# Value products of two key tiles in a row, with sixteen buffers for exponentials, in the attention stages with small heads

## The reference, cut to what matters

```python
scores = jnp.einsum('bhqd,bhkd->bhqk', q, k) * scale      # + mask, or slopes and causal
attn   = jax.nn.softmax(scores, axis=-1)
out    = jnp.einsum('bhqk,bhkd->bhqd', attn, v)
```

## The kernel before, in words

| stage | keys | key tiles `nkt` | small | score banks for the maxima `A_BANKS` |
|---|---|---|---|---|
| pyr_coarse | 512 in blocks of 256, 128, 128 | 4 | yes | 3 |
| pyr_core | 512 | 4 | yes | 3 |
| l1x_core | 1024 | 8 | yes | 3 |
| l2a_core | 512 | 4 | yes | 3 |
| la_core | 1536 | 12 | no | 3 |
| l3a_core | 512, causal | 4 | yes | 3 |
| l3x_core | 1024, masked | 8 | yes | 2 |

## Time and profile before

### The profile page before, as it was taken

The page is one execution under the profiler, slowest core; times in us unless marked ns, Lnnn a source line. Parts: engine busy times, 40 slices in busy tenths (PEclk is TensorE's granted clock), DMA queues, the critical chain, the costliest instruction groups (busy, mean ns, idle before and its releaser), DMA issues. The chain is left out here.

```text
span 5453.5 us, 72915 instructions
## 1 busy us (share of the span) xinstructions
PE 4470.3 (82%) x20471; PEld 2052.5 (38%) x20471; DVE 3008.7 (55%) x6900; ACT 2794.5 (51%) x5841; POOL 1691.7 (31%) x1362
## 2 busy tenths in 40 slices
PE   8779663847799956794898899999998869669986
PEld 5322553745322255323343233333334544312223
DVE  4567564036488522677653555555552247558875
ACT  3447221322366722472444477777774226339993
POOL 2112141121201111121442477777775111300001
PEclk9679876978799977896999899999999889769998
DMA  8544102520823254542545544444430055644421
GB/s 301 137 106 111 54 2 63 189 79 1 283 52 95 56 202 157 175 111 85 184 175 195 128 105 100 102 103 109 109 91 18 34 161 129 206 132 108 109 62 37
DMA packets 534966, 634.87 MB, mean 116 GB/s; under 512 B 84644, under 2 KB 441748, under 8 KB 522180
## 3 DMA queue, kind: packets, MB, share of 16 engines
q1 hardware_dynamic: 527168, 595.62, 38.7%
q0 software_dynamic: 6384, 32.61, 1.9%
q10 hardware_dynamic: 1068, 2.66, 0.2%
HBM read 399.52 MB, written 217.45 MB: 113 GB/s over the span
## 5 line engine op out<-in xcount | busy, mean ns | idle before, releaser
L828 POOL TENSOR_TENSOR la_core_weight_sums<-la_core_weight_sums,la_core_weights 128x1024 f32<-128x1024 f32 x320 | 752.3, 2351 | 140.2 <-ACT la_core_weights L693 132.6
L734 DVE TENSOR_REDUCE la_core_part_max<-ps 128x1 f32<-128x512 f32 x768 | 518.9, 681 | 499.6 <-PE ps L560 499.0
L630 PE MATMUL ps<-la_core_q,la_core_k 128*128 128x512 bf16 x2304 | 624.5, 382 | 13.5 <-ACT ps L676 10.3
L693 ACT ACTIVATE la_core_weights<-ps 128x512 f32<-128x512 f32 x768 | 455.5, 593 | 293.3 <-PE ps L630 293.3
L218 POOL TENSOR_TENSOR proj_parts<-proj_rest,proj_parts 128x512 bf16<-128x512 f32 x240 | 303.8, 1273 | 663.5 <-ACT proj_parts L169 663.0
L676 ACT ACTIVATE ps<-la_core_tops 128x512 f32<-128x512 f32 x768 | 460.3, 599 | 57.9 <-DMA la_core_tops<-la_core_max_rows 57.9
L593 PE MATMUL ps<-la_core_weights,la_core_v 128*64 128x512 f32 x1536 | 414.0, 617 | 0.0
L630 PEld LDWEIGHTS ps<-la_core_q,la_core_k 128*128 128x128 bf16 x2304 | 195.0, 98 | 485.1 <-ACT ps L676 302.5
L734 DVE TENSOR_REDUCE l1x_core_part_max<-ps 128x1 f32<-128x512 f32 x512 | 316.7, 681 | 83.7 <-PE ps L558 77.1
L206 DVE CAST proj_parts<-proj_full 128x512 bf16<-128x512 f32 x240 | 168.0, 700 | 313.8 <-ACT proj_full L181 158.2
L730 DVE CUSTOM_DVE_ANT_0 l3x_core_unused<-ps,l3x_core_mask_q 128x512 f32<-128x512 f32 x512 | 330.6, 686 | 7.4 <-DVE l3x_core_row_max L738 4.9
(11 more groups left out here) (460 smaller groups left out, 8487.2 us busy)
## 6 DMA issues: line engine op xcount, KB each, us to landing
la_core_k<-latent_k_parts SPq DMA_DIRECT2D x128, 384.0 KB
latent_k_parts<-proj_parts SPq DMA_DIRECT2D x96, 384.0 KB, 2.6
cf_w<-in_L1f_w SPq DMA_DIRECT2D x32, 1024.0 KB, 6.9
values<-proj_value SPq DMA_DIRECT2D x112, 256.0 KB, 3.1
latent_values<-proj_value SPq DMA_DIRECT2D x96, 256.0 KB, 3.0
la_core_q<-latent_q_parts SPq DMA_DIRECT2D x192, 128.0 KB
la_core_v<-latent_values SPq DMA_DIRECT2D x32, 768.0 KB, 5.5
k_parts<-proj_parts SPq DMA_DIRECT2D x56, 384.0 KB, 2.6
```

The lines of the kernel that those rows point to most:

```text
L630: mm = nc.tensor.matmul(out, k_stack[r][:, kp, j, ks], q_stack[r][:, p, j, qs], start=False, stop=False, skip_group_check=True)
L693: nc.scalar.activation(weights[:, (g * NS + s) % WEIGHTS, qs], k.ps[:, B0 + (g * NS + s) % B_BANKS, qs], ACT.Exp, scale=scale).then_inc(ex ...
L734: nc.vector.reduce_max(out, scores, AX).then_inc(a_taken, 1)
L828: nc.gpsimd.tensor_tensor(total, total, own, ALU.add).then_inc(added, 1)
```

## The change

In the stages with small heads the value products of two key tiles are issued one behind the other: behind the key tiles 2, 4, 6 of a group stand those of tiles 0 and 1, 2 and 3, 4 and 5, and behind the first key tile of the next group those of its last two tiles. `weights` has 16 buffers there in place of 8, 16 KB more in each partition. `copy_sums` stands behind the second key tile's exponentials in place of the first's. `out_rows` of the pyramid is allocated after pyr_core, and its transfer (256 KB read as a broadcast) moves from the projection before pyr_coarse to SyncE's part of the first level merge, which now waits for it. la_core is as it was.

```diff
-    WEIGHTS = 8
+    WEIGHTS = 16 if small else 8
+    together = 2 if small else 1
     ahead_tiles = WEIGHTS // heads
...
-                    if i:
-                        weigh(b, g, i - 1)
-                    elif exists(*later(b, g, -1)):
-                        weigh(*later(b, g, -1), nkt - 1)
+                    if i and i % together == 0:
+                        for tile in range(i - together, i):
+                            weigh(b, g, tile)
+                    elif i == 0 and exists(*later(b, g, -1)):
+                        for tile in range(nkt - together, nkt):
+                            weigh(*later(b, g, -1), tile)
                     if i == 0 and exists(*later(b, g, 1)):
                         turn(*later(b, g, 1))
...
-            weigh(B - 1, groups - 1, nkt - 1)
+            for tile in range(nkt - together, nkt):
+                weigh(B - 1, groups - 1, tile)
...
-                    if s == heads - 1 and exists(*later(b, g, -1)):
+                    if s == together * heads - 1 and exists(*later(b, g, -1)):
                         copy_sums(*later(b, g, -1))
...
-def merge_levels_stage(k, lvl, att, up, out_w, up_w, out_b, up_b, up_next, value_bias):
+def merge_levels_stage(k, lvl, att, up, out_w, up_w, out_b, up_b, up_next, value_bias, loads=()):
...
         def _(sync):
             k.clear_last_set(sync)
+            for tile, source in loads:
+                sync.dma_start(tile, source).then_inc(loaded, 16)
+            if loads:
+                sync.wait_ge(loaded, 16 * len(loads))
...
-        prefetch += [(out_rows[:], inp["L0_out_b0_up_b0"].partition_broadcast(P)), (out_b[:], inp["L0_out_b"]), (up_b[:], inp["L0_up_b"]),
-                     (vbias[:], inp["L0_v_b"])]
+        prefetch += [(out_b[:], inp["L0_out_b"]), (up_b[:], inp["L0_up_b"]), (vbias[:], inp["L0_v_b"])]
...
+        out_rows = sb("rows", [P, 2, C])
...
-                               up_b[:, min(lvl, 2), :], up[i + 1], vbias[:, lvl, :])
+                               up_b[:, min(lvl, 2), :], up[i + 1], vbias[:, lvl, :],
+                               loads=[(out_rows[:], inp["L0_out_b0_up_b0"].partition_broadcast(P))] if i == 0 else ())
```

More of the change, by code:

```diff
@@ L1023, in merge_levels_stage @@
         nc.sbuf_tensor(f"level_bias_{lvl}", [P, CH], F32) as level_bias,
-        k.stage("values_biased", "bias_sum", "ready", "summed", "quartered", "upsampled") as (
-            values_biased, bias_sum, ready, summed, quartered, upsampled),
+        k.stage("values_biased", "bias_sum", "ready", "summed", "quartered", "upsampled", "loaded") as (
+            values_biased, bias_sum, ready, summed, quartered, upsampled, loaded),
         nc.Block(no_gpsimd_drain=True) as block,
@@ L1088, in pyramid_attention @@
         xs = k.xT[:].rearrange("p c (b s) -> p c b s", b=B)
-        out_w, up_w, out_rows = sb("out_w", [P, 4, CH, C]), sb("up_w", [P, 3, CH, C]), sb("rows", [P, 2, C])
+        out_w, up_w = sb("out_w", [P, 4, CH, C]), sb("up_w", [P, 3, CH, C])
         out_b, up_b = sb("out_b", [P, 4, CH]), sb("up_b", [P, 3, CH])
         prefetch = [(out_w[:, lvl], inp["L0_out_w"][lvl]) for lvl in range(4)] + [(up_w[:, lvl], inp["L0_up_w"][lvl]) for lvl in range(3)]
-        prefetch += [(out_rows[:], inp["L0_out_b0_up_b0"].partition_broadcast(P)), (out_b[:], inp["L0_out_b"]), (up_b[:], inp["L0_up_b"]),
-                     (vbias[:], inp["L0_v_b"])]
+        prefetch += [(out_b[:], inp["L0_out_b"]), (up_b[:], inp["L0_up_b"]), (vbias[:], inp["L0_v_b"])]
         with nc.sbuf_tensor("pyr_wqkv", [P, 4, CH, 3 * C], F32) as w, nc.sbuf_tensor("pyr_zeros", [P, H * QUAD], F32) as zeros:
```

## The result

| | before | after |
|---|---|---|
| median | 5449.86 us (5443.2 to 5451.83, 4 runs) | 5605.7 us (5603.56 to 5611.34, 4 runs) |
| profiled execution | 5453.5 us | 5605.8 us |
| ratio | | 1.0289, 95% interval 1.0275 to 1.0304 |

The change makes the kernel 2.9% slower. The forecast was 5561 us with a range of 5500 to 5600: the direction came as forecast, but the time lies 45 us above the forecast and 6 above the range. The next table sets the terms of the forecast's sum against the two traces; a stage is taken here from the start of its first exponential to the start of its last.

A forecast was written before the change was run, and what follows sets the result against it. TensorE's order was taken as the bound, VectorE close behind, ScalarE in l3x. pyr_core 18, l2a 18, l1x 26, l3x 39, pyr_coarse 4 and l3a 6 give 111 us: 5450 + 111 = 5561 us, range 5500 to 5600.

The forecast's parts named there:

- The bound: Six changed stretches: TensorE's order bounds five, with VectorE 87% full close behind in l1x; ScalarE bounds l3x.
- the switches: On TensorE, switching to value products and back costs 0.24 us; the change saves one in two.
- VectorE's banks: In l1x, eight-pair runs wait for VectorE's three banks: 0.49 us lost, 0.24 saved, so +0.25 us a pair.
- the timetable: l1x chunk starts from the first pass S: last chunk 3.78 us, value products 4.09, next run 5.94.
- Rival 1: Faster: TensorE's order is the bound, only switches count; 160 pairs save 38 us, giving 5412 us; chance 0.07.
- The change of group: A group's first chunk loses its value product cover: pyr_core's pair there +0.98 us, group +1.23; l1x group +1.75.
- Rival 3: The group change costs nothing more, its wait overlapping VectorE's idle time: 5520 us; chance 0.15.
- The term of +39 us: l3x: 1.5 us a group for pairs plus 1.1 at the group change, over 15 groups.
- The last groups, left out: Last two of 16 groups, without pass A: 15 groups counted; range allows up to 2 us for each of 12.
- pyr_coarse and l3a: Additional value products lengthen the wait for the maxima's row: +4 us in pyr_coarse, +6 in l3a.
- The rest at nothing: Exponentials' buffers, `copy_sums` and the moved transfer in the first level merge: 0 us, the transfer at most 2.
- l3x's banks: Upper bound in l3x: VectorE's two banks add another 0.25 us a pair, 15 us more.

The follow-up runs named there:

- VectorE relieved: Changed kernel, VectorE reading only half of each score chunk for its maxima in small-head stages: 5499.47 us; the kernel before with the same halving: 5380.33 us.
- The kernel with single edges: Changed kernel with the value products of a group's last two key tiles issued one at a time, pairs only inside a group: 5524.69 us, ratio 1.0127.
- the kernel that has all fillers: Changed kernel plus redundant score products in l3x: six per group change, two before chunks 8, 16, 24, one behind each last-two-groups pass S product: 5567.0 us.
- the six fillers: Six redundant score products before each l3x group's first pass A chunk: 5586.15 us in the changed kernel, 5454.88 us in the kernel before.
- the relaxed kernel: Changed kernel whose first pass A chunks of a group wait only for the maximum that last used their bank: 5575.03 us, ratio 1.0234.

## Why the prediction was right, and where it was wrong

**The bound, the switches, VectorE's banks: right outside l3x.** Two tiles in a pair take 5.96 us in l1x where they took 5.69, forecast 5.94, and the timetable holds chunk by chunk. With VectorE relieved the pair takes 5.45, which is the switch's 0.24 alone. Rival 1 had the price right and the bound wrong.

**The change of group: right.** 12.83 to 12.92 us in pyr_core (12.9 forecast) and 24.9 to 25.0 in l1x (24.95). The kernel with single edges shows that most of it hangs on the lost cover (0.9 of 1.2 us). Rival 3 falls.

**l3x: this is the step that failed.** The term of +39 us measured +81.9, because the sum priced TensorE's products in l3x at full clock and put the clock's part at nothing. The forecast took "0.5 us a pair, 3 x 0.5 = 1.5 a group" and, at the change of group, "removing that cover of 1.00 adds as much, with some 0.1 more". At full clock both came: 7.47 us a pair, and 31.23 to 31.24 us a group where fillers held the clock. What is missing is the price of waits beyond their own length: two waits of 0.9 us a group became eight of 3.7, and the clock fell to 0.88. Set out with the kernel that has all fillers:

| l3x, us | before | after, all fillers | after |
|---|---|---|---|
| first to last transpose (15 groups) | 441.4 | 478.8 | 509.0 |
| last transpose to last exponential | 54.2 | 58.0 | 68.5 |
| stage | 469.0 | 510.2 | 550.9 |
| clock | 0.97 | 0.98 | 0.88 |

(The first transpose comes 26.6 us ahead of the first exponential in each.) The order is worth 510.2 - 469.0 = 41 us, against 39 forecast; the lost clock 550.9 - 510.2 = 41 us, against none. The split has a fringe: the six fillers cost 4.8 us by themselves in the kernel before, and what the fillers cost after counts here as order. Without any filler, the two groups of the relaxed kernel give about the same price a group: 3.2 us between a clock of 1.00 and one of 0.90. Of the clock's 41 us, 30 lie in the groups with a pass A and 10.5 in the last two groups.

Could it have been seen? The wait of 0.99 us in the earlier trace rows and a granted clock that fell three times in l3x, the last time behind waits of 0.5 to 1.1 us, were both in the trace of before. The forecast itself made the wait of 0.99 into 2.1 us (it measured 1.59), added others behind it, and expected TensorE's busy share to fall, and then priced all products of l3x at the duration they had at full clock.

**The last groups, left out: a smaller miss.** "The last two of 16 groups have no pass A; what they cost there [...] I leave out" was meant to be worth up to 2 us for each such group, so 4 a stage. It was 5 in l1x (41.6 from the last transpose to the last exponential in place of 36.6) and 3.8 in l3x at full clock. Pairs cost there too: 5.27 us in l1x where two tiles took 4.92, 7.53 in l3x where they took 7.0.

**pyr_coarse and l3a: a little too high.** In pyr_coarse the waits for the row rose by 1.0 us in all. pyr_coarse's 31.9 us and l3a's 5.2 became:

```profile
PE ps L627 <- DMA pyr_coarse_q<-pyr_coarse_max_parts: 32.9, 15, 4.4
```

```profile
PE ps L627 <- DMA l3a_core_q<-l3a_core_max_parts: 11.5, 11, 2.7
```

In l3a the wait rose by 6.3 us, as forecast, but the stage only by 2.5, and by 1.1 to 5.9 if the other traces with pairs are set against this one before. Something may have been given back beside the wait. The saved switches are a candidate, which the forecast had ruled out as a gain; no run isolates them there.

**The rest at nothing: right**, as far as 0.15% can show. The kernel with buffers and transfer alone is at 0.9994 (0.9985 to 1.0004).

**The sum.** Of the 42.5 us by which the stages exceed the forecast, l3x has 42.9, l1x 4.1 and pyr_core 1.2; l3a, pyr_coarse and l2a take back 5.4. The upper end of the range allowed 15 us more for l3x's banks and 24 for the last groups, but nothing for the clock. That the total missed the range by only 6 us is due to these allowances, not to a clock that had been counted.

## What to carry to other kernels

A stage that alternates short bursts of products on TensorE with products that need no buffer uses the latter as cover for the buffers of the former; grouping them saves the switch (0.24 us here) and gives away the cover, 1 us a time. When an edit adds waits to TensorE, price the following products at half clock as well, above all in a stage where another engine is the bound and TensorE already has idle time. And count a pipeline's last iterations, in which part of the work is gone, as a case of their own.

## What the runs showed of the hardware

The granted clock fell without a long wait. In a group of l3x with eight waits, the longest 1.30 us, it was 0.90; with the long one relaxed, nine waits of at most 0.51 us and 3.3 us together, it was 0.90 in one group and 1.00 in another. A group of l1x after the change, with a single wait of 1.27 us in 25 us, and one of pyr_core, with 1.11 us in 12.9, kept 1.00. Redundant products in the idle time brought the clock back in steps: with none 0.88 and 550.9 us, with six a group 0.91 and 536.4, with twelve 0.95 and 519.6, with the end of the stage filled too 0.98 and 510.2. They brought nothing where the clock was granted already (473.9 in place of 469.0 us).
